# Seven of eight key rotations moved into the first attention head, and five score banks in the last cross-attention step

## The reference

```python
x = x + xattn(layernorm(x), ctx)      # 8 batches, 16 heads, 1601 context rows each
x = x + attn(layernorm(x), ...)       # 32 query heads, 8 key/value heads of 128
x = x + ffn(layernorm(x), ...)        # inner width 1792, weights rebuilt as below
# attn:
q, k, v = x @ wq.T, x @ wk.T, x @ wv.T            # k and v are used of the first batch only
q, k = apply_rope(q, cos, sin), apply_rope(k, cos, sin)
k_full = concatenate([k_cache[block_idx], k[0]])  # 512 selected keys and 64 new ones
scores = q @ k_full.T / sqrt(128); out = softmax(scores) @ v_full @ wo.T
# ffn weights:  W = mean_w + mean(|w - mean_w|) * sign(w - mean_w)
```

## Time and profile before

| | |
|---|---|
| Median of 3 runs | 888.73 us (888.36 to 892.6) |
| Profiled execution | 887.68 us, span of its instructions 885.7 us |
| PE busy | 845.7 us (95% of the span) |
| DVE, ACT, POOL busy | 609.1, 514.3, 459.1 us |
| Chain that ended last | PE 61%, DVE 2%, POOL 1%, DMA 1% |

### The profile page before, as it was taken

One profiled execution on the slowest core, in us unless ns is written; L12 is line 12 of the kernel. 1 busy time (PEld: TensorE's weight loads), 2 busy tenths in 40 slices (PEclk: granted clock), 3 DMA queues, 4 the chain that ended last, 5 costly groups with the idle time before them and its releaser, 6 DMA issues.

```text
span 885.7 us, 15315 instructions
## 1 busy us (share of the span) xinstructions
PE 845.7 (95%) x5246; PEld 636.2 (72%) x5246; DVE 609.1 (69%) x1002; ACT 514.3 (58%) x989; POOL 459.1 (52%) x294
## 2 busy tenths in 40 slices
PE   6899999999999599999999999999999998899998
PEld 4444555454534488888888888888888887788886
DVE  4755677567647377586775876758758589588773
ACT  4755646464656366565665656656656577455551
POOL 2598798887661343545435444454454543334430
PEclk9899999999999899999999999999999999999999
DMA  9553443204620333060240501505105005255621
GB/s 365 196 207 122 158 176 119 84 7 117 230 107 1 131 117 122 1 214 24 72 164 0 213 24 40 193 4 205 32 5 209 13 1 180 106 174 186 210 71 48
DMA packets 42338, 102.94 MB, mean 116 GB/s; under 512 B 7859, under 2 KB 12979, under 8 KB 41395
## 3 DMA queue, kind: packets, MB, share of 16 engines
q1 hardware_dynamic: 42002, 102.06, 33.0%
q10 hardware_dynamic: 288, 0.26, 0.1%
HBM read 96.95 MB, written 1.05 MB: 111 GB/s over the span
## 4 chain that ended last, share of the span: by engine, by line
PE 61%; DVE 2%; POOL 1%; DMA 1%; SPq 1%; ACT 0%; issue 0%; POOLq 0%; DVEq 0%
PE psum L1528 11%; PE psum L1509 9%; PE psum L1644 9%; PE psum L1582 9%; PE psum L1540 6%; PE psum L1658 4%; PE psum L1567 3%; PE psum L1558 3%; PE psum L1563 3%; PE psum L1549 1%; DMA ffn_raw<-in_L_ffn_mean_w_dram 1%; PE psum L1559 1%; PE psum L1561 1%; SPq L323 1%; POOL head_probs L2015 0%; POOL ffn_raw L2035 0%
## 5 line engine op out<-in xcount | busy, mean ns | idle before, releaser
L2015 POOL TENSOR_TENSOR head_probs<-head_probs,inverse_den 128x576 f32<-128x576 f32 x128 | 147.5, 1153 | 203.3 <-DVE inverse_den L1872 203.3
L1201 DVE TENSOR_REDUCE max_part<-psum 128x1 f32<-128x804 f32 x128 | 121.2, 990 | 50.6 <-PE psum L753 50.2
L1065 ACT ACTIVATE probs<-psum 128x512 f32<-128x512 f32 (+1 forms) x208 | 106.8, 608 | 57.5 <-PE psum L775 56.9
L1756 ACT ACTIVATE head_probs<-psum,neg_max 128x576 f32<-128x576 f32 x128 | 94.7, 740 | 54.2 <-DVE neg_max L1889 53.5
L1889 DVE TENSOR_REDUCE neg_max<-psum 128x1 f32<-128x576 f32 x128 | 96.9, 757 | 23.3 <-PE psum L1528 22.0
L623 POOL TENSOR_TENSOR prob_sums<-prob_sums,probs 128x1024 f32<-128x1024 f32 (+1 forms) x42 | 100.2, 2385 | 7.2 <-ACT probs L1065 2.7
L1528 PE MATMUL psum<-k_high,query_t_high 128*128 (+1 forms) x256 | 87.1, 340 | 2.8 <-POOL value_low L2044 2.8
L623 POOL TENSOR_TENSOR prob_sums<-probs 128x1024 f32<-128x1024 f32 x30 | 71.3, 2381 | 33.0 <-ACT probs L1065 32.9
L1540 PE MATMUL psum<-ident,head_probs 128*128 128x128 f32 x496 | 78.9, 275 | 7.8 <-POOL head_probs L2015 6.5
L1865 DVE TENSOR_TENSOR probs_t_low<-psum,probs_t_high 128x512 fp32r<-128x512 f32 x124 | 84.7, 683 | 1.0
L2035 POOL TENSOR_TENSOR ffn_quant<-ffn_raw 128x1536 f32<-128x1536 f32 x13 | 45.6, 3512 | 68.5 <-DVE ffn_w_low L1951 26.9
(11 more groups left out here) (242 smaller groups left out, 1903.3 us busy)
## 6 DMA issues: line engine op xcount, KB each, us to landing
ctx_t_odd<-in_ctx_dram SPq DMA_DIRECT2D x4, 3202.0 KB, 10.7
ffn_raw<-in_L_ffn_w_dram SPq DMA_DIRECT2D x42, 256.0 KB, 3.9
ffn_raw<-in_L_ffn_mean_w_dram SPq DMA_DIRECT2D x42, 256.0 KB, 4.2
w_piece<-in_L_ffn_w_dram SPq DMA_DIRECT2D x21, 512.0 KB, 6.5
w_piece<-in_L_ffn_mean_w_dram SPq DMA_DIRECT2D x21, 512.0 KB, 7.8
cache<-in_ctx_dram SPq DMA_DIRECT2D x3, 3202.0 KB, 10.5
wq_nat<-in_L_attn_wq_dram SPq DMA_DIRECT2D x32, 256.0 KB, 7.4
wo_nat<-in_L_attn_wo_dram SPq DMA_DIRECT2D x32, 256.0 KB, 3.2
```

Of the source, the lines that this page charges most:

```text
L1065: act.activation(prob_buffer(b, t)[0:rows, half * BANK:(half + 1) * BANK], psum[0:rows, n % SCORE_BANKS, :], ACT.Exp, scale=XSCALE).then_i ...
L1201: dve.tensor_reduce(max_part[:, qt, pair:pair + 1], psum[:, bank:bank + 2, 0:PIECE_KEYS], AX.XY, ALU.max).then_inc(s_max, 1)
L1756: act.activation(probs[:, qt, :].rearrange("p (a k) -> p a k", a=2), psum[:, 2 * (qt % 2):2 * (qt % 2) + 2, 0:HALF], ACT.Exp, bias=neg_max ...
L2015: pool.tensor_tensor(probs[:, qt, :], probs[:, qt, :], rden[:, qt:qt + 1].to_broadcast([P, KEYS]), ALU.mult).then_inc(s["norm"], 1)
```

## The change

Three things change.

1. In the last step of the cross-attention the scores from tile 2 on go round five PSUM banks (0, 1, 2, 5, 7) instead of three. The order is changed with it: `mix` of the batch before comes ahead of tile 4, and `values` takes two units at a time.
2. Only the rotation of key/value head 0 stays in the join. The other seven matmuls stand in head 0 of the attention: one behind each of its four tiles of scores, three behind its queries. Their copies on ACT and DVE stand in head 0 too. The banks are 4, 5, 6 in turn, and head 1 waits for all low parts. `first_queries` no longer waits for rotations, but for the last mix. SP waits for all eight rotations before it goes on from the first feed-forward loads, since later loads overwrite the cache.
3. POOL takes `difference(0)` behind its four divisions of head 1 and no longer ahead of head 0.

```diff
@@ -335,6 +335,7 @@
 RING, SUMS = 8, 6
 HALVES = 2 * KT
 SCORE_BANKS = 3
+LAST_BANKS = (0, 1, 2, 5, 7)
 U_BANK = 3
 C_COPIES = 3 * (GROUPS + 1)
 C_WIDTH = MAIN + TAIL
 
+def score_bank(b, t, half):
+
+    n = 2 * t + half
+    if b + 1 < BATCH or n < 4:
+        return (HALVES * b + n) % SCORE_BANKS
+    return LAST_BANKS[(n - 1) % len(LAST_BANKS)]
+
+
-ROTATED_BANK = (3, 4, 6, 7, 3, 4, 1, 2)
+ROTATED_BANK = (3,) + (4, 5, 6) * 2 + (4,)
+def rotate_back(core, pe, g, done):
+    selected = core.cache[:, 0].rearrange("p t c -> p (t c)").rearrange("p (n g k) -> p n g k", n=TOPK, g=NKV)
+    pe.matmul(core.psum[:, ROTATED_BANK[g], :].rearrange("p (n k) -> p n k", n=TOPK), core.rope[:, :],
+              selected[:, :, g, :], start=True, stop=True).then_inc(done, 1)
...
+
+
+def rotated_low(core, dve, g, k_high, k_low, high, done):
+    dve.wait_ge(high, g + 1)
...
@@ -769,10 +791,10 @@
                 for half in range(2):
                     n = HALVES * b + 2 * t + half
 
-                    wait(pe, s_exp, n - SCORE_BANKS + 1)
+                    wait(pe, s_exp, n + 1 - (len(LAST_BANKS) if b + 1 == BATCH and t >= 2 else SCORE_BANKS))
                     if t == 0:
                         pe.wait_ge(s_shift, 2 * b + half + 1)
-                    pe.matmul(psum[0:rows_of(t), n % SCORE_BANKS, :], lhs,
+                    pe.matmul(psum[0:rows_of(t), score_bank(b, t, half), :], lhs,
                               rhs[:, half * BANK:(half + 1) * BANK], start=True, stop=True).then_inc(s_sb, 1)
@@ -806,22 +828,23 @@
 
             def last_step(b):
 
+                pe.wait_ge(s_cnat, BATCH)
+                pe.wait_ge(s_shift, 2 * BATCH)
                 scores(b, 2)
                 scores(b, 3)
-                values(b, range(0, 1))
+                mix(b - 1)
                 scores(b, 4)
-                mix(b - 1)
                 scores(b, 5)
-                values(b, range(1, 2))
-                for u in range(2, UNITS - 2):
-                    scores(b, 2 * u + 2)
-                    scores(b, 2 * u + 3)
-                    values(b, range(u, u + 1))
-                    if u == 3:
-                        pe.wait_ge(s_d, 2 * b)
-                        denominator_round(b, (0, 1), True)
+                values(b, range(0, 2))
+                for t in range(6, 10):
+                    scores(b, t)
+                values(b, range(2, 4))
+                scores(b, 10)
+                scores(b, 11)
+                pe.wait_ge(s_d, 2 * b)
+                denominator_round(b, (0, 1), True)
                 scores(b, KT - 1)
-                values(b, range(UNITS - 2, UNITS - 1))
+                values(b, range(4, 6))
                 denominator_round(b, (2, 3), False)
                 last_tail(b)
@@ -1008,23 +1031,8 @@
                                       core.ident[:, :])
                 mm.then_inc(s_kturn, 1)
 
-            def rotate_back(g):
-                if g == 0:
-                    pe.wait_ge(core.cache_in, 2 * TOPK * 16)
-                    pe.wait_ge(s_step, 6)
-                elif g == 2:
-                    pe.wait_ge(s_mix, BATCH)
-                elif g == 3:
-                    pe.wait_ge(s_vcopy, 4)
-                elif g in (4, 5):
-                    pe.wait_ge(s_lo, g - 3)
-                elif g in (6, 7):
-                    pe.wait_ge(norm2.s_low, g - 4)
-                pe.matmul(psum[:, ROTATED_BANK[g], :].rearrange("p (n k) -> p n k", n=TOPK), core.rope[:, :],
-                          selected[:, :, g, :], start=True, stop=True).then_inc(s_back, 1)
-
...
             new_tokens(NEW_VALUE_BANK, kv["wv"]).then_inc(s_newv, 1)
-            rotate_back(0)
+            pe.wait_ge(core.cache_in, 2 * TOPK * 16)
+            pe.wait_ge(s_step, 6)
+            rotate_back(core, pe, 0, s["back"])
+            turn_new_keys()
             pe.wait_ge(norm2.s_low, 1)
             norm2.tile_turn(pe, 3)
-            rotate_back(1)
-            turn_new_keys()
-            for g in range(2, NKV):
-                rotate_back(g)
...
@@ -1470,6 +1460,7 @@
             for i in range(REP):
                 load_output_weight(core, qo, sp, 0, i)
             load_ffn_weights(core, raw[0], s_raw[0], sp, 0)
+            sp.wait_ge(s["back"], NKV)
             with sp.Fori(1, NKV) as g:
                 for i in range(REP):
 
@@ -1583,12 +1574,18 @@
                                        start=(i == 0 and step == 0), stop=(i == REP - 1 and step == 2))
                 mm.then_inc(s["o"], 1)
 
+            def other_keys(k):
+                wait(pe, s["lo"], k - 2 if k > 3 else 0)
+                rotate_back(core, pe, k, s["back"])
+
             vl_at = [None]
 
             def head(g, i, this, last, nxt):
                 n = REP * g + i
                 vl_at[0] = 2 * g + (2 if i else 0)
 
+                if isinstance(g, int) and n == 1:
+                    pe.wait_ge(s["lo"], NKV)
                 for qt in range(TT):
                     if nxt and qt in QUERY_PARTS:
                         if qt == 2:
@@ -1601,8 +1598,13 @@
                         turn_probs(g, i, qt)
                     if this:
                         score(g, n, qt)
+                    if isinstance(g, int) and n == 0:
+                        other_keys(qt + 1)
                 if nxt:
                     queries(i + 1, QUERY_PARTS[TT])
+                if isinstance(g, int) and n == 0:
+                    for k in range(TT + 1, NKV):
+                        other_keys(k)
 
                 if last:
@@ -1725,8 +1729,13 @@
                     turned_high(g, i, TT - 1)
                 if this:
                     exponential(n, TT - 1)
+                if isinstance(g, int) and n == 0:
+                    rotated_high(core, act, TT, k_high, s["back"], s["hi"])
                 if nxt:
                     queries_high(i + 1, n + 1)
+                if isinstance(g, int) and n == 0:
+                    for k in range(TT + 1, NKV):
+                        rotated_high(core, act, k, k_high, s["back"], s["hi"])
                 if nxt and has_weight(g, i):
                     query_weight_high(g + (i + 2) // REP, (i + 2) % REP)
                 if this and i > 0:
@@ -2017,6 +2033,8 @@
                 if i == 1 and last and not (isinstance(g, int) and g == 0):
                     pool.wait_ge(s_abs, 3 * g + 1)
                     pool.tensor_tensor(total[:, :], total[:, :], part[:, :], ALU.add).then_inc(s_tot, 1)
+                if isinstance(g, int) and n == 1:
+                    difference(0)
                 if i == 0:
                     wait(pool, s["pv"], n)
                     values(g)
@@ -2044,8 +2062,6 @@
             pool.memset(value[1][SEQ:P, ST, :].bitcast(F32), 0.0).then_inc(s["vz"], 1)
             pool.wait_ge(s["vz"], 1)
             pool.wait_ge(core.cache_in, 2 * TOPK * 16)
-            pool.wait_ge(s["wql"], 2)
-            difference(0)
             run(pool, head)
             for c in range(1, CH):
                 difference(c)
```

More of the change, by code:

```diff
@@ L1065, in exponential @@
                     act.activation(prob_buffer(b, t)[0:rows, half * BANK:(half + 1) * BANK],
-                                   psum[0:rows, n % SCORE_BANKS, :], ACT.Exp, scale=XSCALE).then_inc(s_exp, 1)
+                                   psum[0:rows, score_bank(b, t, half), :], ACT.Exp, scale=XSCALE).then_inc(s_exp, 1)
             def compressed(b):
@@ L1895, in head @@
                         invert(n, qt - 1)
+                    if isinstance(g, int) and n == 0 and qt > 0:
+                        rotated_low(core, dve, qt, k_high, k_low, s["hi"], s["lo"])
                     if qt == TT - 1 and last:
@@ L1903, in head @@
                     invert(n, TT - 1)
+                if isinstance(g, int) and n == 0:
+                    rotated_low(core, dve, TT, k_high, k_low, s["hi"], s["lo"])
                 if nxt:
                     queries_low(i + 1, n + 1)
+                if isinstance(g, int) and n == 0:
+                    for k in range(TT + 1, NKV):
+                        rotated_low(core, dve, k, k_high, k_low, s["hi"], s["lo"])
                 if nxt and has_weight(g, i):
```

37 lines of the change are left out of this document (13 added, 24 removed).

## The result

The changed kernel took 880.84 us (median of 4 runs, 880.29 to 881.48) against 888.55 us for the kernel before (median of 4, 888.19 to 892.6). The ratio is 0.991, with a 95% interval of 0.988 to 0.9935: 0.93% faster, where 0.55% was forecast. The direction was right. The profiled execution of the changed kernel took 881.48 us, with a span of 879.6.

A forecast was written before the change was run, and what follows sets the result against it. PE's own work was taken to bound the kernel, so only its waits or low clock could give. 2.5 + 4.4 + 2.1 - 2.4 - 1.7 = 4.9 us gained: 882.8 profiled, 883.8 against the median; range 880.5 to 886.5.

The forecast's parts named there:

- A: Last batch step: five banks let PE run further ahead of ACT; 2.5 us gained, capped by POOL at 2.8.
- B: Join: seven rotations leave it, but first queries then wait for the last tile of tokens; 4.4 us gained.
- C: Heads 0 and 1: rotations lengthen head 0 to 15.3 us, the 6.5 and 1.1 us waits go; 2.1 us gained.
- D: Head 2: POOL's moved difference holds up DVE's low parts of weights, so PE stands; 2.4 us lost.
- E: Head 2: PE's granted clock falls behind the 2.4 us gap; 1.7 us lost, bounds 0 and 1.7.
- The first rival: Head 2: the clock does not fall behind the 2.4 us gap; 882.1 us, chance 0.20.
- The slower rival: Head 0: the clock stays low throughout, costing 12.2 us instead of 1.7; 894.3 us, chance 0.07.
- the one with falls at every small gap: Gaps of 1.5, 2.8, 1.5 and 2.4 us: two more clock falls cost 3.4 us; 887.2 us, chance 0.13.

## Why the prediction was right or wrong

- **A, last step:** right. 2.52 us against 2.5, two gaps of ACT of the forecast size, POOL close behind at 268.0. Confirmed with the part alone and with the part taken out.
- **B, join:** right, 4.24 against 4.4. PE waited 1.50 us for the last tokens' low part, as worked out.
- **C, heads 0 and 1:** right, with some luck. 15.27 us to head 1 (15.3 forecast), and 2.06 us in all. But the 15.3 counts the fall ahead of head 0 as certain, and four of eleven profiles have none; with the rotations in head 0 it then took 13.65 or 13.66 us. Nor does the prediction say which move takes the 6.5 us wait away: either does it alone.
- **D, the difference:** right in cause and size: 2.33 us against 2.4, and one wait of POOL removes it. The sum has the difference run from 322.55 to 325.9, 3.35 us, where its own row has 3.51; with that it would give 2.55. In the changed kernel POOL ended at 318.04, 3.34 us behind the end of `wq_t_low` at 314.70, so the shorter time was the better one. Its shape was not right. I had one gap at the third transposition, and it is two, at the queries and there, with 0.7 us of matmuls between.
- **E, the clock behind D: this step failed.** "The nearest row to a PE gap of 2.4 us is the 2.8 us one, which cost 1.7 us of clock" priced one long gap at its full cost. The gap came as 1.35 and 0.56 us and no profile of four shows a fall behind it. So the term was 0 us where 1.7 were counted. The first rival, without that fall, is what happened, though not for its reason, which still supposed one gap of 2.4 us. Even for a gap that did come as 2.2 us the row was no price but one outcome of two. And in the kernel before the 1.7 us were no loss of time at all, since the 6.5 us wait behind them hid them. What a fall costs where nothing hides it was 1.6 us in the long head 0.
- **From the profile to the median.** The forecast missed the median by 883.8 - 880.84 = 3.0 us. Of this E is 1.7. The small errors of A to D take 0.1 off it, and what differed ahead of the step and behind head 3 (0.99 lost, 0.70 gained) takes 0.3. The rest, 1.7 us, is the reference: before's profiled execution lay 1.05 us below the median shown, which I added, and after's lies 0.64 above its own. Single executions of these kernels differ by 1 us and more, and that both differences pointed the same way here is chance.
- The slower rival and the one with falls at every small gap are refuted for these runs: no fall behind the waits of 1.50 and 1.41 us either (`PEclk` 1.00 from 283 to 288 and from 304 to 308 us), and the clock was back at 1.00 by 295 us, inside head 0.

What stays open is what decides between fall and no fall behind the same 2.0 to 2.8 us. The profiles show both with the same code and the same waits ahead of the gap. The 1.50 us wait ahead of the 2.8 us gap doesn't decide it either: with it there were five falls in seven profiles, without it (the rotations in the join) two in four. It was not tried to hold the clock up through such a gap with other matmuls.

## What to carry to other kernels

When two edits both cover one wait, time each alone: here they brought 4.4 and 5.6 us, but 4.0 together, and the best version left one of them out. Before a long POOL instruction is put into a stretch, look there for DVE instructions with two SBUF inputs and place it behind them; one wait was worth 2.3 us in its stretch. Price a fall of the clock as a chance, from several profiles, not as a cost read from one row, and give the range its width.

## What the runs showed of the hardware

- The granted clock behind a PE gap of 2.0 to 2.8 us varied from execution to execution: seven falls of eleven behind 2.8 us, one of two behind 2.20, one of two behind 2.0. A fall ahead of head 0 cost 1.0 us with the short head 0 (9.35 against 8.36), 1.6 with the long one (15.27 against 13.66), and nothing where PE waited for POOL behind it (14.24 against 14.29).
- POOL and DVE took turns at two-SBUF-input instructions in both directions: POOL's difference took 3.93 us when DVE's `wq_t_low` ran as it was issued and 3.49 when nothing did. With a short subtraction added behind it, the pair of low parts took 5.41 us and not 4.57, and POOL's subtraction 1.37 us where a third of 3.49 is 1.16.
- In the last step with three banks PE and ACT fell into one of two rhythms, 23.7 or 25.2 us for the same code. ACT's gaps in the slower one, in the kernel with the difference alone moved:

```profile
255.76 1.09 ACT L1065 ACTIVATE probs<-psum 128x512 f32<-128x512 f32 x2 [1.84 <-PE psum L775]
257.68 1.09 ACT L1065 ACTIVATE probs<-psum 128x512 f32<-128x512 f32 x2 [0.83 <-PE psum L775]
259.33 2.06 ACT L1065 ACTIVATE probs<-psum 128x512 f32<-128x512 f32 x4 [0.56 <-PE psum L775]
```

The ten profiles with five banks show one rhythm, 21.18 to 21.20 us. With three banks there are only three profiles, so how often the slower one comes isn't known.
